# Cross-attention and expert layer on one core: overflow in groups of 64 slots, two tiles a step, second product on quarters of the array

## The chip, the cores and the metric

The kernel runs on one core of a Trainium2 chip. The metric is the device time of one execution in microseconds. Before the change the median of three runs is 230.85 us (230.7 to 230.89).

## The reference

The input x is 4 sequences of 256 tokens with 256 features, so N = 1024 tokens. It first gets an attention-like term of 256 columns added. Then comes the layer that this change is about, on z, the normalised x:

```
logits = z @ Wr.T + 0.5 * dom            # 64 experts
_, topk_idx = top_k(logits + router_bias, 4)
combine = softmax scores of the chosen four, scaled to sum 1
g, u = z @ Wg[e], z @ Wu[e]              # 256 -> 64, each expert e
out  = sum over e of (silu(g) * u * combine[:, e]) @ Wd[e]
for i in range(2): out += (silu(z @ Sg[i]) * (z @ Su[i])) @ Sd[i]   # shared, 256 -> 256 -> 256
```

Each token goes to four of the 64 experts, so there are 4096 pairs of token and expert, 64 an expert on average. Everything is float32.

## The kernel before

The attention term, the normalisations, the transposed z (`zT`), the logits and the choice of experts come first (up to about 50 us of the trace). In that time SP's queue brings in all expert weights. `codes`, `one_hot`, `list_tokens` and `tokens` then turn the choices into lists of tokens, one column of 128 slots for each tile. Each round of a list is one `one_hot` on VectorE (DVE), one `value` on ScalarE (ACT) and eight products on TensorE (PE, line 987).

A tile is 128 rows of z. There are two kinds:

- 32 *pair* tiles (NP). Slots 0 to 63 hold the first 64 tokens of expert 2q, slots 64 to 127 those of expert 2q + 1.
- *Overflow* tiles for what an expert has beyond 64 tokens, each 128 slots of one expert, whose number is known only at run time. They run in turns of four (U).

What a tile goes through, in the function `step` of each engine:

- POOL gathers its rows from `z_rows` in DRAM into `xg`, a ring of four (line 362 for pairs, 374 for overflow).
- PE transposes them in two pieces (line 1017). DVE copies them to `xgT` (line 810).
- PE multiplies by gate and up weights: line 1050 for a pair, in which each expert uses one half of the array's columns, line 1054 for overflow, on the whole array, with the expert's number in a register. Each float32 product is two instructions.
- ACT makes the silu (line 499). DVE multiplies by the up part (line 824, or 829 with the expert's parity, so that the right half of two stacked `wd` matrices is hit).
- PE transposes h (lines 1073, 1075), ACT copies it to `hT` (line 508), and PE makes the second product of 256 columns (line 1086).
- ACT copies y to `ysb`, a ring of four (line 518), and SP stores it to `y_slots` (lines 285, 291).

`over_tiles` writes the order out by hand: in one step the engines transpose tile s, do gate/up of tile s-1, turn h of tile s-2 and do the second product of tile s-3. The first 32 + 8 steps are written out, the others are a loop. Other work is put into certain steps: the second list of tokens for overflow (steps 1 to 12), `pick_choice` on DVE (line 773, two a step in steps 13 to 28).

When all y are stored, POOL gathers the 32 sets of result rows (`y_slots` to `z`, line 394, ring of eight), and DVE adds each with its weight (line 864). Beside this PE does the rest of the shared experts: `unit` (line 928) and `shared_out` (line 1122). Two of eight units are done before the tiles. SP stores the result in eight pieces.

## Time and profile before

| | |
|---|---|
| median of 3 runs | 230.85 us |
| span of the profiled execution, first to last instruction | 213.5 us |
| what lies around the span, against the median | 17.35 us |
| PE busy in the span | 173.6 us |
| POOL busy | 111.2 us |
| pair tiles, overflow tiles | 32, 28 |

The profiled execution is shown by its span alone; the runs are timed without it, and their median stands beside the span. Times in the trace count from the span's start. A row of a timeline is a start, a duration and a group of merged instructions; matmuls are pipelined and their ends modelled, so the distance between starts tells what the engine spends. "issue" is idle time that no recorded event explains. PEclk gives the granted clock of PE in tenths of full speed.

### The profile page before, as it was taken

To read this page: it belongs to the slowest core of one execution; us is meant where nothing else is said; L and a number is where in the kernel's file an instruction comes from. 1 tells how busy PE (TensorE), PEld (TensorE's weight loads), DVE (VectorE), ACT (ScalarE), POOL (GpSimd) and SP (SyncE) were. 2 spreads that over 40 slices of the span, in tenths; PEclk is the share of its full clock that TensorE was granted. 3 is DMA by queue.
4 is the path that set the end of the run, shared out by engine and by line. 5 is a ranking of instruction groups with operands and counts; after the bars stand their busy time and mean duration, and the time that the engine had idled before them with its cause. 6 is when DMAs were issued, how large, how long until landed. Compare 5 with 4: busy or idle time off the path is not lost.

```text
span 213.5 us, 4117 instructions
## 1 busy us (share of the span) xinstructions
PE 173.6 (81%) x963; PEld 124.0 (58%) x965; DVE 133.0 (62%) x528; ACT 88.4 (41%) x270; POOL 111.2 (52%) x121
## 2 busy tenths in 40 slices
PE   0990288999889999999999979999989979978300
PEld 0460178735536887777778968888844367436200
DVE  2999970467877655998997746666531440486450
ACT  2627496416224664555555636555551110210000
POOL 6595110010276535666665766666303777677740
PEclk9999999999655999999999999999999999999975
DMA  6899999997023432455544343443322333344431
GB/s 141 242 384 350 350 352 366 380 365 259 2 75 93 119 112 87 134 155 145 146 129 126 112 133 88 136 125 104 120 98 74 101 98 98 87 127 142 124 119 66
DMA packets 29825, 34.50 MB, mean 162 GB/s; under 512 B 4248, under 2 KB 27561, under 8 KB 29680
## 3 DMA queue, kind: packets, MB, share of 16 engines
q1 hardware_dynamic: 25392, 25.90, 36.8%
q0 software_dynamic: 4416, 8.41, 15.2%
q8 instruction: 7, 0.11, 0.3%
q14 instruction: 10, 0.08, 0.1%
HBM read 27.99 MB, written 9.96 MB: 178 GB/s over the span
## 4 chain that ended last, share of the span: by engine, by line
PE 66%; DVE 13%; ACT 6%; issue 4%; POOL 4%; DMA 3%; SPq 1%; POOLq 1%; DVEq 0%; ACTq 0%
PE pb L1086 13%; PE pb L928 13%; PE pb L1050 10%; PE pb L1017 7%; PE pb L1054 6%; PE pb L1073 4%; PE pb L1122 3%; POOL z L394 3%; PE pb L987 3%; DMA xs<-in_x 2%; PE pb L1075 2%; DVE sc L563 2%; DMA z<-y_slots,slot_i 1%; ACT z L428 1%; DVE sc L557 1%
## 5 line engine op out<-in xcount | busy, mean ns | idle before, releaser
L362 POOL DMA_INDIRECT xg<-z_rows,tok x32 | 32.9, 1029 | 29.3 <-issue 11.6
L394 POOL DMA_INDIRECT z<-y_slots,slot_i x32 | 32.5, 1016 | 21.4 <-DMA y_slots<-ysb 11.3
L1086 PE MATMUL pb<-wd_sb,hT 128*128 128x256 f32 (+1 forms) x120 | 37.5, 396 | 0.0
L374 POOL DMA_INDIRECT xg<-z_rows,tok_now x28 | 27.9, 997 | 14.3 <-issue 11.5
L928 PE MATMUL pb<-zT,shared_sb 128*128 128x512 f32 x64 | 32.3, 658 | 0.7 <-ACT ysb L518 0.7
L810 DVE COPY xgT<-pb 128x256 f32<-128x256 f32 x60 | 25.3, 422 | 11.4 <-PE pb L1017 10.4
L518 ACT ACTIVATE ysb<-pb 128x256 f32<-128x256 f32 x60 | 23.0, 383 | 12.1 <-PE pb L1086 11.1
L1017 PEld LDWEIGHTS pb<-ident,xg 128*128 128x128 f32 x120 | 22.6, 198 | 8.3 <-issue 5.1
L1017 PE MATMUL pb<-ident,xg 128*128 128x128 f32 x120 | 25.3, 294 | 1.9 <-issue 1.3
L499 ACT ACTIVATE sg<-pb 128x64 f32<-128x64 f32 x60 | 13.4, 223 | 29.8 <-PE pb L1050 18.9
L1050 PE MATMUL pb<-wgu_sb,xgT 128*64 128x128 f32 x256 | 22.4, 299 | 0.3 <-DVE xgT L810 0.3
L864 DVE SCALAR_TENSOR_TENSOR xs<-z,wgt,xs 128x256 f32<-128x256 f32 x32 | 15.4, 482 | 10.6 <-DMA z<-y_slots,slot_i 8.7
L928 PEld LDWEIGHTS pb<-zT,shared_sb 128*128 128x128 f32 x64 | 12.8, 206 | 15.5 <-issue 15.3
L1086 PEld LDWEIGHTS pb<-wd_sb,hT 128*128 128x128 f32 x120 | 19.9, 206 | 1.7 <-issue 0.6
L829 DVE SCALAR_TENSOR_TENSOR hh<-sg,parity,pb 128x64 f32<-128x64 f32 x56 | 13.2, 277 | 9.5 <-ACT sg L499 9.0
L469 ACT ACTIVATE qkT<-pb 128x512 f32<-128x512 f32 x8 | 4.8, 597 | 33.6 <-PE pb L928 33.6
L1122 PE MATMUL pb<-shared_sb,hsh 128*128 128x256 f32 x64 | 14.6, 384 | 4.3 <-DVE hsh L794 2.8
L1054 PE MATMUL pb<-wgu_sb,xgT 128*128 x112 | 17.7, 280 | 0.0
L824 DVE TENSOR_TENSOR hh<-sg,pb 64x64 f32<-64x64 f32 x64 | 13.9, 217 | 5.9 <-ACT sg L499 4.1
L508 ACT ACTIVATE hT<-pb 128x128 f32<-128x128 f32 x60 | 16.5, 276 | 2.4 <-PE pb L1075 1.0
L1050 PEld LDWEIGHTS pb<-wgu_sb,xgT 128*64 128x64 f32 x256 | 14.2, 144 | 4.9 <-DVE xgT L810 1.2
L1122 PEld LDWEIGHTS pb<-shared_sb,hsh 128*128 128x128 f32 x64 | 11.9, 190 | 7.8 <-DVE hsh L794 4.5
(165 smaller groups left out, 242.0 us busy)
## 6 DMA issues: line engine op xcount, KB each, us to landing
wgu_sb<-in_wgu SPq DMA_DIRECT2D x8, 1024.0 KB, 10.9
y_slots<-ysb SPq DMA_DIRECT2D x60, 128.0 KB
wd_sb<-in_wd SPq DMA_DIRECT2D x4, 1024.0 KB, 12.0
shared_sb<-in_shared SPq DMA_DIRECT2D x1, 1536.0 KB, 9.7
xs<-in_x SPq DMA_DIRECT2D x4, 256.0 KB, 4.4
z_rows<-z SPq DMA_DIRECT2D x4, 256.0 KB, 9.0
out<-xs SPq DMA_DIRECT2D x8, 128.0 KB, 1.8
xg<-z_rows,tok POOLq DMA_INDIRECT x32, 3.0
```

What stands on the lines that cost most here:

```text
L362: g.indirect_dma_start(xg[:, n, :], None, z_dram, bass.IndirectOffsetOnAxis(ap=tok[:, t:t + 1], axis=0), bounds_check=N - 1, oob_is_err=Fa ...
L374: g.indirect_dma_start(xg[:, n, :], None, z_dram, bass.IndirectOffsetOnAxis(ap=tok_now[:, n:n + 1], axis=0), bounds_check=N - 1, oob_is_er ...
L394: g.indirect_dma_start(z[:, j % NC, :].bitcast(I32), None, y_dram, bass.IndirectOffsetOnAxis(ap=slot_i[:, 0, j:j + 1].bitcast(U32), axis=0 ...
L508: a.activation(hT[:, n, :], pb[7][:, 0:P], ACT.Identity).then_inc(hT_sb, 1)
L518: a.activation(ysb[:, n, :], pb[4 + m % 2][:, 0:D], ACT.Identity).then_inc(y_sb, 1)
L810: v.tensor_copy(xgT[:, n, :, :], pb[n][:, 0:D].rearrange("p (c n) -> p c n", c=DC)).then_inc(xT_sb, 1)
L928: ins = t.matmul(pb[2 * (n % 2) + g][:, :], sgu_sb[:, i, g, h, hc * P:(hc + 1) * P], zT[:, h, blk * 512:(blk + 1) * 512], start=(h == 0), ...
L1017: ins = t.transpose(pb[n][:, h * P:(h + 1) * P], xg[:, m, h::DC], ident[:, :])
L1050: ins = t.matmul(pb[2 + n][h, 0:2 * F], xgT[:, n, c, h], wgu_sb[:, 2 * q + g, c, :], start=(c == 0), stop=(c == DC - 1))
L1054: ins = t.matmul(pb[2 + n][:, 0:2 * F], xgT[:, n, h, :], wgu_sb[:, bass.ds(gu_of[k], 1), h, :].rearrange("p o f -> p (o f)"), start=(h == ...
L1086: t.matmul(pb[4 + n][:, 0:D], hT[:, n, :], wd_sb[:, q, :] if pair else wd_sb[:, bass.ds(d_of[k], 1), :].rearrange("p o d -> p (o d)"), sta ...
L1122: ins = t.matmul(pb[4 + i % 4][:, 0:D], hsh[:, q, i * P:(i + 1) * P], sd_sb[:, q, :], start=(q == 0), stop=(q == NSH * DC - 1))
```

## The change

- Overflow is counted in groups of 64 slots. An overflow tile holds two groups, each of its own expert, so that it has the same form as a pair tile. `parity` and the dynamic weight addresses on PE are gone. Instead the weights of a group's expert are loaded again from DRAM into a place of `w_sb` whose own expert is done. SP does that: in each of the first 18 double steps it loads two experts, 0.197 MB each.
- Gate/up weights and the second weights lie together in one tensor `w_sb` of 384 numbers an expert and partition. `Wd` is stored with its left 128 columns in partitions 0 to 63 and its right 128 columns in 64 to 127.
- Tiles are done two at a time (a double step d, ND2 = 24 of them written out: 16 of pairs, 8 of overflow). Then a loop of turns of two tiles, at least one. In step d PE does gate/up of d, transposes of d+2, the second product of d-1 and the turn of h of d. The loop's turns have no such staging.
- h is written twice side by side, so that its transpose stands in both halves of the partitions. The second product is done in quarters: 64 rows by 64 columns of the array each, 128 moving columns, four for a tile.
- y of two tiles is stored by one DMA of 256 KB, from a ring of three.
- The list of overflow tokens is made for 32 tiles in place of 64. Shared experts, result gathers and the final additions stay as they are.

Of the loops' bodies only the added lines are shown; the removed ones stand in the kernel above.

```diff
-MAXOV = 64
+OT = 16
+MAXOV = 32
+NG = 2 * MAXOV
+ND2 = (NP + OT) // 2
...
-U = 4
-HEAD = 2
-XB = 4
-YB = 4
-GU_LAG, D_LAG = 1, 3
+XD = 3
+XB = 2 * XD
+YD = 3
+GROUP_W = DC * 2 * F + D // 2
+G0, G1 = 0, DC * 2 * F
...
-        wgu_sb = sb("wgu_sb", [P, E, DC, 2 * F])
-        wd_sb = sb("wd_sb", [P, E // 2, D])
+        w_sb = sb("w_sb", [P, E, GROUP_W])
+        wgu_v = w_sb[:, :, G0:G1].rearrange("p e (c n) -> p e c n", c=DC)
...
+        xgT = sb("xgT", [P, 2, 2, DC, P])
+        sg = sb("sg", [P, 2, 2, F])
+        hh = sb("hh", [P, 2, 2, 2, F])
+        hT = sb("hT", [P, 2, 2, P])
+        ysb = sb("ysb", [P, YD, 2, D])
+        tok_now = sb("tok_now", [P, 2], U32)
...
+                sp.dma_start(w_sb[:, 8 * n:8 * (n + 1), :], w[8 * n:8 * (n + 1), :, :].rearrange("e p n -> p e n")).then_inc(ld_w[n], 16)
...
+            def store(at, ring):
+                return sp.dma_start(y_dram[at, :].rearrange("(i p) d -> p i d", p=P), ysb[:, ring, :, :].bitcast(I32))
+            def experts_of(place):
+                _, vals = nc.values_load_multi_w_load_instructions(
+                    group_e[0:1, place], engines=[mybir.EngineType.SP], min_val=0, max_val=E - 1,
+                    skip_runtime_bounds_check_because="VectorE has bounded the expert of every group by E - 1")
+                return list(vals)
+            def reload(entry, expert):
+                return sp.dma_start(w_sb[:, entry, :], w[bass.ds(expert, 1), :, :].rearrange("o p n -> p (o n)"))
+            for d in range(ND2):
+                sp.wait_ge(y_sb, d + 1)
+                store(slice(2 * d * P, 2 * (d + 1) * P), d % YD).then_inc(y_out[d % YD], 16)
+                if d == 0:
+                    sp.wait_ge(at_ok, 2)
+                if d < OT + 2 and d % 2 == 0:
+                    pair = experts_of(slice(2 * d, 2 * d + 4))
+                if d < OT + 2:
+                    for h in range(2):
+                        reload(2 * d + h, pair[2 * (d % 2) + h]).then_inc(ld_over[d // 2], 16)
             n_turns = turn_count(sp)
             with sp.Fori(0, n_turns) as turn:
+                sp.wait_ge(y_sb, turn + (ND2 + 1))
+                store(bass.ds(turn * (2 * P) + 2 * ND2 * P, 2 * P), ND2 % YD).then_inc(y_out[ND2 % YD], 16)
+                later = experts_of(bass.ds(turn * 4 + (2 * OT + 4), 4))
+                for h in range(4):
+                    reload(2 * OT + h, later[h]).then_inc(ld_over[OT // 2], 16)
+            sp.wait_ge(mixed, K)
+            sp.wait_ge(ld_over[OT // 2], n_turns * 64 + 64)
...
-            g.memset(tri_less[:, :], float(P)).then_inc(const_ok, 1)
+            g.memset(tri_less[:, :], float(HB)).then_inc(const_ok, 1)
...
-            for t in range(NP):
+            for t in range(2 * ND2):
                 n = t % XB
                 if t >= XB:
-                    pool.wait_ge(xT_ps, t - XB + 1)
-                g.indirect_dma_start(xg[:, n, :], None, z_dram, bass.IndirectOffsetOnAxis(ap=tok[:, t:t + 1], axis=0),
+                    pool.wait_ge(xT_ps, t // 2 - XD + 1)
+                if t == NP:
+                    pool.wait_ge(tok_step, 5)
+                which = tok[:, t:t + 1] if t < NP else tok_over[:, t - NP:t - NP + 1]
...
+            pool.wait_ge(xT_ps, ND2 - XD + 1)
+            turn_no = ctx.enter_context(pool.register("turn_no"))
+            pool.reg_mov(turn_no, 1)
             n_turns = turn_count(pool)
+            with pool.Fori(0, n_turns) as _:
+                pool.wait_ge(tok_set, turn_no)
+                pool.reg_add(turn_no, turn_no, 1)
+                for i in range(2):
+                    n = 2 * (ND2 % XD) + i
+                    g.indirect_dma_start(xg[:, n, :], None, z_dram, bass.IndirectOffsetOnAxis(ap=tok_now[:, i:i + 1], axis=0),
+                                         bounds_check=N - 1, oob_is_err=False).then_inc(got[n], 16)
+            for n in range(YD):
+                more = n_turns * 16 if n == ND2 % YD else 0
+                pool.wait_ge(y_out[n], more + 16 * ((ND2 - 1 - n) // YD + 1))
+            last_row = n_turns * (2 * P) + (2 * ND2 * P - 1)
...
+            def gate(d, n):
+                act.wait_ge(gu_ps, d + 1)
+                a.activation(sg[:, n, :, :], pb[2 + n][:, 0:4 * F].rearrange("p (i f) -> p i f", i=2)[:, :, 0:F], ACT.Silu).then_inc(silu_ok, 1)
+            def evac_hT(d, n):
+                act.wait_ge(hT_ps, d + 1)
+                a.activation(hT[:, n, :, :], pb[2 + n][:, 256:512].rearrange("p (i n) -> p i n", i=2), ACT.Identity).then_inc(hT_sb, 1)
+            def evac_y(d, ring):
+                act.wait_ge(y_ps, d + 1)
+                for i in range(2):
+                    ins = a.activation(ysb[:, ring, i, :].rearrange("p (h c) -> p h c", h=2), banks[:, 4:6, i * P:(i + 1) * P], ACT.Identity)
+                ins.then_inc(y_sb, 1)
+            for d in range(ND2):
+                if d >= 2:
+                    act.wait_ge(h_ok, d - 1)
+                gate(d, d % 2)
+                if d >= 1:
+                    if d > YD:
+                        act.wait_ge(y_out[(d - 1) % YD], 16 * ((d - 1) // YD))
+                    evac_y(d - 1, (d - 1) % YD)
+                if d >= 2:
+                    act.wait_ge(y_ps, d - 1)
+                evac_hT(d, d % 2)
+                if d < NR:
+                    value(d, MAXOV, NR)
+            act.wait_ge(y_out[(ND2 - 1) % YD], 16 * ((ND2 - 1) // YD))
+            evac_y(ND2 - 1, (ND2 - 1) % YD)
+            n_turns = turn_count(act)
+            with act.Fori(0, n_turns) as turn:
+                d, n, ring = turn + ND2, ND2 % 2, ND2 % YD
+                act.wait_ge(h_ok, d)
+                gate(d, n)
+                act.wait_ge(y_ps, d)
+                evac_hT(d, n)
+                act.wait_ge(y_out[ring], turn * 16 + 16 * (ND2 // YD))
+                evac_y(d, ring)
...
-                v.tensor_scalar(need[:, 0, :], pb[5][0:E, 0:P], 1.0 / P, 0.5 - (0.5 + HB) / P, ALU.mult, ALU.add).then_inc(need_ok, 1)
+                v.tensor_scalar(need[:, 0, :], pb[5][0:E, 0:P], float(HB), -HB + 0.5 * HB - 0.5, ALU.max, ALU.add).then_inc(need_ok, 1)
                 dve.wait_ge(need_ok, 1)
-                v.tensor_scalar(need_bf[:, :], need[:, 0, :], ROUND, -ROUND, ALU.add, ALU.add).then_inc(need_ok, 1)
+                v.tensor_scalar(need[:, 1, :], need[:, 0, :], 1.0 / HB, ROUND, ALU.mult, ALU.add).then_inc(need_ok, 1)
+                dve.wait_ge(need_ok, 2)
+                v.tensor_scalar(need_bf[:, :], need[:, 1, :], -ROUND, None, ALU.add).then_inc(need_ok, 1)
...
+                v.tensor_scalar(turns_f[:, :], pb[5][0:1, 260:261], 0.25, 0.375 - OT / 2, ALU.mult, ALU.add).then_inc(turns_step, 1)
...
+            def group_experts():
                 dve.wait_ge(expert_ps, 1)
                 dve.wait_ge(at_ok, 1)
+                v.tensor_scalar(group_e[:, 0:NG], pb[7][0:1, 0:NG], float(E - 1), None, ALU.min).then_inc(at_ok, 1)
...
+            def evac_xT(d, n):
+                dve.wait_ge(xT_ps, d + 1)
+                v.tensor_copy(xgT[:, n, :, :, :].rearrange("p i c n -> p (i c n)"), pb[n][:, :]).then_inc(xT_sb, 1)
+            def hidden(d, n):
+                dve.wait_ge(silu_ok, d + 1)
+                up = pb[2 + n][:, 0:4 * F].rearrange("p (i f) -> p i f", i=2)[:, :, F:2 * F]
+                for k in range(2):
+                    ins = v.tensor_tensor(hh[:, n, :, k, :], sg[:, n, :, :], up, ALU.mult)
+                ins.then_inc(h_ok, 1)
+            evac_xT(0, 0)
+            evac_xT(1, 1)
+            for d in range(ND2):
+                if d >= 2:
+                    dve.wait_ge(hT_ps, d - 1)
+                hidden(d, d % 2)
+                if d + 2 < ND2:
+                    dve.wait_ge(gu_ps, d + 1)
+                    evac_xT(d + 2, d % 2)
+                if d == 0:
+                    group_experts()
+                if d < NR:
+                    one_hot(d, MAXOV, lanes, NR, NP)
+                if d == NR:
                     dve.wait_ge(lexp_ok, 1)
                     dve.wait_ge(z_out, 16 * B)
                     v.tensor_reduce(zden[:, 0, :], logit[:, :, :], AX.X, ALU.add).then_inc(w_step, 1)
                     tokens(tok_over[:, 0:MAXOV], pb[6][:, 192:192 + MAXOV], MAXOV, 2 * NR, 3)
                     dve.wait_ge(tok_step, 5)
+                    v.tensor_copy(tok_now[:, :], tok_over[:, OT:OT + 2]).then_inc(tok_set, 1)
+                if NR < d <= NR + NJ // 2:
+                    pick_choice(2 * (d - NR - 1))
+                    pick_choice(2 * (d - NR - 1) + 1)
+                if d == NR + NJ // 2 + 1:
                     weights_of_choices()
+            n_turns = turn_count(dve)
+            with dve.Fori(0, n_turns) as turn:
+                d, n = turn + ND2, ND2 % 2
+                dve.wait_ge(gu_ps, d)
+                evac_xT(d, n)
+                v.tensor_copy(tok_now[:, :], tok_over[:, bass.ds(turn * 2 + (OT + 2), 2)]).then_inc(tok_set, 1)
+                dve.wait_ge(hT_ps, d)
+                hidden(d, n)
...
+            def split_x(d, n, ring):
+                for i in range(2):
+                    for h in range(DC):
+                        ins = t.transpose(pb[n][:, (i * DC + h) * P:(i * DC + h + 1) * P], xg[:, 2 * ring + i, h::DC], ident[:, :])
+                ins.then_inc(xT_ps, 1)
+            def gate_up(d, n, entry):
+                for i in range(2):
+                    for c in range(DC):
+                        for h in range(2):
+                            own = slice(h * HB, (h + 1) * HB)
+                            ins = t.matmul(pb[2 + n][own, i * 2 * F:(i + 1) * 2 * F], xgT[:, n, i, c, own], wgu_v[:, entry + 2 * i + h, c, :],
+                                           start=(c == 0), stop=(c == DC - 1), skip_group_check=True)
+                ins.then_inc(gu_ps, 1)
+            def turn_h(d, n):
+                for i in range(2):
+                    ins = t.transpose(pb[2 + n][:, 256 + i * P:256 + (i + 1) * P], hh[:, n, i, :, :].rearrange("p k f -> p (k f)"), ident[:, :])
+                ins.then_inc(hT_ps, 1)
+            def down(d, n, entry):
+                for i in range(2):
+                    for h in range(2):
+                        own = slice(h * HB, (h + 1) * HB)
+                        for r in range(2):
+                            rows = slice(r * HB, (r + 1) * HB)
+                            ins = t.matmul(pb[4 + r][own, i * P:(i + 1) * P], hT[rows, n, i, own], w_sb[rows, entry + 2 * i + h, G1:],
+                                           start=True, stop=True, skip_group_check=True)
+                ins.then_inc(y_ps, 1)
+            def entry_of(d):
+                return 4 * d if d < NP // 2 else 4 * d - 2 * NP
+            def x_here(d):
+                for i in range(2):
+                    pe.wait_ge(got[2 * (d % XD) + i], 16 * (d // XD + 1))
             pe.wait_ge(unit_sb, 2)
+            x_here(0)
+            split_x(0, 0, 0)
+            x_here(1)
+            split_x(1, 1, 1)
+            pe.wait_ge(unit_sb, 2 * EARLY)
+            for d in range(ND2):
+                pe.wait_ge(xT_sb, d + 1)
+                if d >= 2:
+                    pe.wait_ge(hT_sb, d - 1)
+                if d < NP // 2:
+                    if d % 2 == 0:
+                        pe.wait_ge(ld_w[d // 2], 16)
+                else:
+                    pe.wait_ge(ld_over[d - NP // 2], 64)
+                gate_up(d, d % 2, entry_of(d))
+                if d + 2 < ND2:
+                    x_here(d + 2)
+                    split_x(d + 2, d % 2, (d + 2) % XD)
+                if d >= 1:
+                    pe.wait_ge(hT_sb, d)
+                    if d >= 2:
+                        pe.wait_ge(y_sb, d - 1)
+                    down(d - 1, (d - 1) % 2, entry_of(d - 1))
+                pe.wait_ge(h_ok, d + 1)
+                turn_h(d, d % 2)
+                if d == 0:
                     pe.wait_ge(cmp_ok, 2)
+                    pe.wait_ge(slot_ok, 1)
+                    t.matmul(pb[7][0:1, 0:NG], ones_bf[0:E, 0:1], cmp[:, :], start=True, stop=True,
                              skip_group_check=True).then_inc(expert_ps, 1)
+                if 1 <= d <= NR:
+                    list_tokens(d - 1, MAXOV, NR, 192)
+            pe.wait_ge(hT_sb, ND2)
+            pe.wait_ge(y_sb, ND2 - 1)
+            down(ND2 - 1, (ND2 - 1) % 2, entry_of(ND2 - 1))
+            n_turns = turn_count(pe)
+            with pe.Fori(0, n_turns) as turn:
+                d, n = turn + ND2, ND2 % 2
+                for i in range(2):
+                    pe.wait_ge(got[2 * (ND2 % XD) + i], turn * 16 + 16 * (ND2 // XD + 1))
+                pe.wait_ge(xT_sb, d)
+                split_x(d, n, ND2 % XD)
+                pe.wait_ge(ld_over[OT // 2], turn * 64 + 64)
+                pe.wait_ge(hT_sb, d)
+                pe.wait_ge(xT_sb, d + 1)
+                gate_up(d, n, 2 * OT)
+                pe.wait_ge(h_ok, d + 1)
+                turn_h(d, n)
+                pe.wait_ge(turns_step, 3)
+                pe.wait_ge(hT_sb, d + 1)
+                pe.wait_ge(y_sb, d)
+                down(d, n, 2 * OT)
+            end = n_turns + ND2
+            pe.wait_ge(xT_sb, end)
+            pe.wait_ge(hT_sb, end)
...
+                if blk == 0:
+                    pe.wait_ge(y_sb, end)
...
+        "w": np.concatenate([np.stack([L0_ffn_Wg.reshape(E, P, DC, F), L0_ffn_Wu.reshape(E, P, DC, F)], 3).reshape(E, P, -1),
+                             L0_ffn_Wd.reshape(E, F, 2, D // 2).transpose(0, 2, 1, 3).reshape(E, P, -1)], 2),
```

## Rows read from the trace of the kernel before

**Rows 1.** The page: busy time, clock by 40 slices, chain by engine.
```profile
PE 173.6 (81%) x963; PEld 124.0 (58%) x965; DVE 133.0 (62%) x528; ACT 88.4 (41%) x270; POOL 111.2 (52%) x121
...
PEclk9999999999655999999999999999999999999975
...
PE 66%; DVE 13%; ACT 6%; issue 4%; POOL 4%; DMA 3%; SPq 1%; POOLq 1%; DVEq 0%; ACTq 0%
```
**Rows 2.** Timeline of PE, 52 to 78 us: start, us, line, instructions merged into a row.
```profile
54.48 1.48 PE L987 MATMUL pb<-oh_val,sc 128*128 128x32 f16 x16 [0.62 <-DVE oh_tile L685]
...
62.70 1.12 PE L1050 MATMUL pb<-wgu_sb,xgT 128*64 128x128 f32 x8 [0.28 <-DVE xgT L810]
...
69.96 1.13 PE L987 MATMUL pb<-oh_val,sc 128*128 128x64 f16 x8
70.92 0.40 PE L1017 MATMUL pb<-ident,xg 128*128 128x128 f32 x2
71.25 0.66 PE L1050 MATMUL pb<-wgu_sb,xgT 128*64 128x128 f32 x8
71.83 0.33 PE L1073 MATMUL pb<-ident,hh 128*128 128x128 f32 x1
72.00 0.60 PE L1086 MATMUL pb<-wd_sb,hT 128*128 128x256 f32 x2
72.43 0.39 PE L1017 MATMUL pb<-ident,xg 128*128 128x128 f32 x2
```
**Rows 3.** Timeline of PE, 154 to 162 us.
```profile
154.24 0.27 PE L1075 MATMUL pb<-ident,hh 128*128 128x128 f32 x1
154.35 0.60 PE L1086 MATMUL pb<-wd_sb,hT 128*128 x2
154.78 0.39 PE L1017 MATMUL pb<-ident,xg 128*128 128x128 f32 x2
155.01 0.61 PE L1054 MATMUL pb<-wgu_sb,xgT 128*128 x4
155.46 0.27 PE L1075 MATMUL pb<-ident,hh 128*128 128x128 f32 x1
...
160.25 1.96 PE L928 MATMUL pb<-zT,shared_sb 128*128 128x512 f32 x4 [0.67 <-ACT ysb L518]
```
**Rows 4.** Timeline of POOL: the first gather of x and three gathers of results.
```profile
57.39 1.23 POOL L362 DMA_INDIRECT xg<-z_rows,tok  x1 [10.07 <-DVE tok L694]
...
162.98 1.00 POOL L394 DMA_INDIRECT z<-y_slots,slot_i  x1 [11.26 <-DMA y_slots<-ysb]
164.28 0.99 POOL L394 DMA_INDIRECT z<-y_slots,slot_i  x1 [0.30 <-issue]
...
204.66 0.99 POOL L394 DMA_INDIRECT z<-y_slots,slot_i  x1 [0.30 <-issue]
```
**Rows 5.** Groups by line, 80 to 116 us: busy us, mean ns of one, idle before.
```profile
L824 DVE TENSOR_TENSOR hh<-sg,pb 64x64 f32<-64x64 f32 x46 | 10.0, 217 | 2.7 <-ACT sg L499 1.5
L810 DVE COPY xgT<-pb 128x256 f32<-128x256 f32 x23 | 9.7, 423 | 2.3 <-PE pb L1017 1.7
...
L518 ACT ACTIVATE ysb<-pb 128x256 f32<-128x256 f32 x23 | 8.8, 383 | 3.6 <-PE pb L1086 3.6
...
L773 DVE SCALAR_TENSOR_TENSOR z<-slotmap,slot,logit 128x64 f32<-128x64 f32 x32 | 7.9, 282 | 0.5
...
L499 ACT ACTIVATE sg<-pb 128x64 f32<-128x64 f32 x24 | 5.4, 223 | 12.1 <-PE pb L1050 12.1
```
**Rows 6.** DMA queues, 92 to 112 us: packets, MB, share of 16 engines.
```profile
q0 software_dynamic: 649, 1.08, 25.2%
q1 hardware_dynamic: 1875, 1.71, 25.0%
```
**Rows 7.** DMA queue of SP, 14 to 50 us, the same columns.
```profile
q1 hardware_dynamic: 12871, 13.02, 109.0%
```
**Rows 8.** The chain in order of time: start, us, what.
```profile
125.46 1.32 issue
```

279 lines of the change are left out of this document (18 added, 261 removed).

## The prediction

> **What bounds the kernel now.** I began with the page. PE is busy 81% of the span and carries 66% of the chain that ended last; its clock digits are low only between about 59 and 75 us [rows 1]. The clock falls while PE waits around the listing of tokens, and comes back some microseconds after the expert tiles have begun.
>
> Then the timeline of PE. It shows three stretches after the routing. From 62.7 us on [rows 2] 32 pair tiles run, each two experts of 64 slots; then 28 overflow tiles of one expert each; from 160.25 us on [rows 3] the shared expert's products. In both tile stages PE has no real gap, so a tile costs what PE spends on it. One full-clock pair tile is the stretch from 70.92 to 72.43 us [rows 2]: starts 0.33, 0.58, 0.17 and 0.43 us apart, 1.51 us together. One overflow tile is 154.24 to 155.46 us [rows 3]: 0.11, 0.43, 0.23, 0.45, together 1.22 us. The second is easy to read: a float32 product is two instructions, 4 of 128 columns take 0.45 us and 2 of 256 take 0.43, so 128 columns are a slot of 0.107 us; a transpose is one slot. 11 slots are 1.18 us and 0.04 us is left over. The pair tile has 8 gate/up instructions of 128 columns on 64 columns of the array. One after the other they would take 0.86 us alone; they start within 0.58 us. So the two halves of the array work side by side: 4 slots, 0.43 us. The tile is again 11 slots, 1.18 us, and the other 0.33 us is the price of going from the whole array to halves and back.
>
> Behind PE, at nearly the same pace, stands POOL. Its gathers cannot follow each other faster than every 1.30 us (162.98 and 164.28) [rows 4]. And the end of the kernel hangs on POOL too: the 32 gathers of results begin at 162.98 us, once the last tile is stored, the last starts at 204.66 [rows 4], and the span ends 8.8 us after that. PE's own last stage runs beside them. So I take it that the end moves by what the first result gather moves.
>
> **The number of tiles.** Routing the reference's inputs gives 27 overflow tiles of 128 slots (before runs them in turns of 4, hence 28) and 35 groups of 64. After runs 16 overflow tiles, 32 groups, in the written-out part and one turn of two tiles for the other 3. That is 50 tiles for 60: 24 double steps and one turn.
>
> **One double step on PE.** Gate/up: 16 instructions in 8 side-by-side slots, 0.86 us. Four transposes of x: 0.43. Two of h: 0.21. The second product is 16 instructions of 128 columns on quarters of the array. Before shows no quarter. Serial they are 16 slots, 1.71 us; as halves 8 slots, 0.86; all four side by side 4 slots, 0.43. The half-array rows [rows 2] overlap fully and here the row halves write to different banks, so I take 0.43. The order halves, whole, quarters, whole has four changes, twice a pair tile's two: 0.66 us. Sum 2.59 us, against 3.02 for two pair tiles and 2.44 for two overflow tiles: per tile the overflow stage gains nothing; the gain is the 10 tiles and, in the pair stage, half of the second product.
>
> What may stand in the way of it in a step:
> - h. From the end of gate/up to the turn of h lie: 0.2 us until ACT starts, a silu of 128 elements (0.22 for 64, I take 0.28), two DVE products of 128 elements (0.22 each for 64, 0.54 together) and some 0.15 of handing over, 1.17 us. PE has 1.12 us of other work meanwhile (transposes, second product, changes). Some 0.1 us stays open: 2.70 us.
> - POOL: 2 gathers, 2.60 us, just under. The ring of three double tiles lets it run ahead.
> - DVE: copy of 512 columns 0.69 (0.42 for 256), products 0.54, two choices 0.72 [rows 5]: under 2.0 us. ACT: 0.28, two y copies of 0.38 and one of h, under 1.5 us [rows 5]. Both hidden by PE, with over half a microsecond of cover.
> - DMA. In the pair stage stores and gathers take 25.0% and 25.2% of the engines [rows 6], which is 1.52 us in the 3.02 us of two tiles. Added are, for the first 18 double steps, two expert blocks of 197 KB. The first loads bring 13.02 MB in 36 us, 362 GB/s [rows 7]; so 1.09 us. Together 2.61 us. That is a third resource at the same pace, and full. Reloads share SP's queue with the stores: a late store holds back ACT three steps on, then PE. The loads themselves are not wanted for 8 steps or more. I put the wait at 0 to 0.4 us a step and take nothing, as the double step is 0.1 longer than the demand.
> - SP: per step a store and two reloads instead of two stores, and it waits for each step's y first; nobody but its own queue stands behind that wait. Reading four expert numbers every other step is hidden.
>
> **The beginning.** Before starts gate/up at 62.70 us, after the first two gathers (57.39 us on). After transposes two double tiles first, so four gathers must have landed: the fourth starts about 4 us after the first and lands 3 us later, 65 us. With four transposes at half clock gate/up begins at about 66 us. The first two steps run wholly or mostly at half clock (gate/up 1.7 us, everything else doubled), as in before the rise came 5 to 6 us after 62.7. Adding them up I get the gate/up of the third double tile at about 75 us; before had then begun its seventh tile (about 75.2). So the start costs one double tile, near 3 us. Token listing: 4 rounds of 8 products, 0.96 us for 64 columns (69.96 to 70.92) and some 0.7 for 32 (54.48, 16 in 1.48) [rows 2]; three lie behind 75 us, 2.1 us.
>
> **The end.** 75.0 + 22 x 2.70 + 2.1 + 1.2 (the last second product, no longer covered) = 137.7 us. The turn isn't pipelined: each engine reads the count, which cost PE 1.32 us of issue at the old loop's start [rows 8], I take 1.0; transposes 0.43, copy 0.9, gate/up 0.96, silu 0.5, products 0.64, h 0.3, its copy 0.6, second product 0.53, y copies 0.96: 6.8 us. Then 3.2 us for a store twice as large (about 3.0 now) until the first result gather, at 147.7 us. Before: 162.98. Gain 15.3 us. The reference is the profile's span of 213.5 us; the median of the runs, 230.85 us, lies 17.35 us above it, which I leave as it is: 198.2 + 17.35 = 215.5 us. Ends for each unknown: per 0.1 us of step 2.2 us; second product between 0.43 and 0.86, up to +9.5 us (serial 1.71, +28); DMA wait up to 0.4 on 16 steps, +6.4; beginning +-2; turn 5 to 8 us.
>
> **Rivals.**
> 1. *The second product overlaps only in halves, or the weights of four quarters load in turn.* Step 3.13 us, so +9.5: 225 us. For: there are as many weight loads as products, and 4 of each would have to start within 0.107 us. Against: in the half-array stretch the loads start in pairs too. Chance 0.14.
> 2. *DMA is the bound while reloading.* Loads, stores and gathers together may move less than each alone: 3.05 us for 16 steps, 221 us. For: the demand of 2.61 us, and no stretch of before has all three at full share. Against: nothing needs these loads soon. Chance 0.15.
> 3. *Slower: the supply of PE instructions.* After has 38 weight loads and 38 products a double step, before 26 of each for two pair tiles in 3.02 us, that is 116 ns a couple; an overflow tile has 9 in 1.22 us. If 116 ns were the pace at which they can be supplied, a step would be 4.4 us and the kernel 37 us above my forecast, 253 us. It turns to a loss from a step of 3.4 us, 89 ns a couple. Against it: 8 couples start inside 0.58 us [rows 2], 73 ns each, and gaps stand only where the array mode changes. But those eight may have waited in a queue; no row shows 38 on end. Chance 0.08. A milder pace between 73 and 89 ns, say 3.08 us a step or 224 us, has 0.06. Serial quarters (step 3.98, 244 us) would end on the slow side too, chance 0.03.
> The Trainium skill bears on this place (TensorE: Matmul & The Clock Gate, Back-to-back issue gap): a lasting stream of loads and products of 128 columns is given as about 81 ns each. By that, an estimate from that page, 38 would be 3.08 us and the time some 224 us, the milder pace above; the half-array row beats it for eight, and no row tests it for longer.
> 4. *Better than forecast.* Some changes of mode hide, or the start loses nothing: POOL's 2.60 us then holds: 211 us. Chance 0.1.
>
> **Chances.** The forecast, a step of 2.6 to 2.85 us, 212 to 219 us: 0.44. All but rival 3 at its full price and serial quarters are faster than before. The range 210 to 227 takes in the forecast, rivals 1 and 2, the milder pace and most of 4; outside are rival 3, serial quarters and a rest of mishaps. A measurement can tell about 0.2%, 0.5 us, from no change; faster by more 0.87, within it 0.02, slower 0.11.
>
> **What would show it.** Second product: 16 instructions starting within 0.43 to 0.5 us (0.9 means rival 1). Double steps 2.7 us apart at full clock between 80 and 135 us; evenly longer with gaps before gate/up too is rival 3, longer only up to the 18th step with ACT or POOL waiting on DMA is rival 2. POOL's gathers close to 1.3 us apart all through. First result gather near 148 us and the same 50 us from there to the end. I am wrong if the tail grows, if the turn drops PE's clock for the shared expert's products, or if the first steps at half clock last longer than to 75 us.

## The result, and the profile after

| occasion | before | after | ratio, 95% interval |
|---|---|---|---|
| first comparison | 230.77 us (4 runs) | 220.32 us (219.29 to 221.47, 4 runs) | 0.9552, 0.95 to 0.9605 |
| fourth | 227.53 us | 217.78 us | 0.9541, 0.9456 to 0.9627 |
| sixth | 228.08 us | 218.36 us | 0.9619, 0.9559 to 0.9679 |

The kernel is 10.45 us faster where 15.35 was forecast. Sign and range (210 to 227 us) held, though 220.32 lies above the 212 to 219 of the forecast itself; the way to it did not hold. The span of the profiled execution of after is 218.0 us where the forecast's sum gave 198.2. What lies around the span is 2.0 us where the sum carried 17.35. So two errors, 19.8 us one way and 15.3 us the other, stood against each other, and that the time still lies in the range is luck.

The page of after, first its busy times, then the clock in 40 slices, then the chain by engine (answers to [rows 1]):

```profile
PE 153.2 (70%) x1245; PEld 104.9 (48%) x1246; DVE 105.0 (48%) x388; ACT 68.1 (31%) x190; POOL 101.6 (47%) x111
...
PEclk9999999999958889999999999999859999999755
...
PE 48%; DVE 13%; issue 10%; another core or an unknown queue 9%; ACT 8%; POOL 5%; DMA 5%; POOLq 1%; DVEq 0%; ACTq 0%
```

PE is down from 81% to 70% of a longer span: a kernel that PE bounded is now idle for a fifth of the stage of the double steps (PE busy 35.04 us of 45 between 80 and 125 us). The clock isn't the reason; the granted clock is 1.00 from 81 to 152 us. Where PE is not waiting, its parts are what the forecast said. The timeline of PE near the end of the stage (start, us, line; answers to [rows 2, 3]), and then the turn:

```profile
144.63 1.10 PE L1005 MATMUL pb<-w_sb,xgT 128*64 128x128 f32 x16
145.66 0.75 PE L996 MATMUL pb<-ident,xg 128*128 128x128 f32 x4
146.34 0.67 PE L1022 MATMUL pb<-w_sb,hT 64*64 64x128 f32 x16
146.93 0.44 PE L1012 MATMUL pb<-ident,hh 128*128 128x128 f32 x2
147.30 1.09 PE L1005 MATMUL pb<-w_sb,xgT 128*64 128x128 f32 x16
...
152.88 0.67 PE L1022 MATMUL pb<-w_sb,hT 64*64 64x128 f32 x16 [0.53 <-ACT hT L493]
154.54 0.74 PE L996 MATMUL pb<-ident,xg 128*128 128x128 f32 x4 [0.99 <-issue]
156.06 1.77 PE L1005 MATMUL pb<-w_sb,xgT 128*64 128x128 f32 x16 [0.78 <-DVE xgT L800]
158.79 0.69 PE L1012 MATMUL pb<-ident,hh 128*128 128x128 f32 x2 [0.96 <-DVE hh L807]
160.06 1.13 PE L1022 MATMUL pb<-w_sb,hT 64*64 64x128 f32 x16 [0.58 <-issue]
```

Gate/up 1.03 us, transposes 0.68, the second product on quarters 0.59 for 16 instructions, the turn of h 0.37: 2.67 us. But this step is an exception, and it stands behind the last gather of rows, which starts at 143.22 us. A dozen steps before it, all engines of one step in order of time:

```profile
100.74 1.00 POOL L362 DMA_INDIRECT xg<-z_rows,tok  x1 [1.34 <-PE pb L996]
...
101.29 1.09 PE L1005 MATMUL pb<-w_sb,xgT 128*64 128x128 f32 x16
...
102.04 1.00 POOL L362 DMA_INDIRECT xg<-z_rows,tok  x1 [0.30 <-issue]
...
102.32 0.75 PE L996 MATMUL pb<-ident,xg 128*128 128x128 f32 x4
...
103.00 0.67 PE L1022 MATMUL pb<-w_sb,hT 64*64 64x128 f32 x16
103.67 0.28 ACT L488 ACTIVATE sg<-pb 128x128 f32<-128x128 f32 x1 [1.83 <-PE pb L1005]
...
104.05 0.49 DVE L807 TENSOR_TENSOR hh<-sg,pb 128x128 f32<-128x128 f32 x2 [2.18 <-ACT sg L488]
104.41 1.00 POOL L362 DMA_INDIRECT xg<-z_rows,tok  x1 [1.37 <-PE pb L996]
...
104.59 0.44 PE L1012 MATMUL pb<-ident,hh 128*128 128x128 f32 x2 [0.93 <-DVE hh L807]
104.96 0.77 PE L1005 MATMUL pb<-w_sb,xgT 128*64 128x128 f32 x10
```

The step takes 3.67 us (101.29 to 104.96). PE leaves gate/up at about 102.4, yet ACT's silu starts at 103.67 and is said to have waited for exactly that. The recorded semaphore events show why: the increment at the end of gate/up lands at 103.59 us, those of the transposes and of the second product at 103.65 and 103.81. All come out together, 1.2 us late for the first. I call this a **late signal**: a group of matmuls whose increment is recorded over 0.1 us after its last matmul has ended. The counts below match increments with matmuls and can be off by some four, since records are missing. In this profile 45 of 66 are late between 80 and 140 us. In the profile of before that the forecast rests on it is 0 of 225 from 66 to 155 us. No increment of ACT or DVE is late in any profile in that stretch. In after itself the late signals end with the gathers of rows: from 145.7 to 165.9 us, between the last of these gathers and the first result gathers, none of 16 is late.

The end of the kernel, POOL's timeline (answers to [rows 4]), and the DMA queues from 92 to 112 us (answers to [rows 6]):

```profile
165.16 1.00 POOL L389 DMA_INDIRECT z<-y_slots,slot_i  x1 [20.94 <-DMA y_slots<-ysb]
...
190.04 1.19 POOL L389 DMA_INDIRECT z<-y_slots,slot_i  x1 [4.32 <-DVE xs L852]
...
210.02 1.00 POOL L389 DMA_INDIRECT z<-y_slots,slot_i  x1 [0.30 <-issue]
```

```profile
q1 hardware_dynamic: 3266, 3.82, 57.7%
q0 software_dynamic: 524, 0.95, 22.8%
```

The first result gather comes at 165.16 us, forecast 147.7. From there to the end it is 52.8 us, forecast 50.5; a stall of 4.3 us stands in it, in which POOL waits for DVE, DVE for ACT and ACT for the shared expert's products. PE and ACT of after there, then the same of before:

```profile
181.09 7.03 PE L916 MATMUL pb<-zT,shared_sb 128*128 128x512 f32 x16
188.06 1.08 ACT L464 ACTIVATE qkT<-pb 128x512 f32<-128x512 f32 x2 [14.75 <-remote]
```

```profile
179.21 10.46 PE L928 MATMUL pb<-zT,shared_sb 128*128 128x512 f32 x24
182.84 0.60 ACT L469 ACTIVATE qkT<-pb 128x512 f32<-128x512 f32 x1 [11.42 <-PE pb L928]
```

The first eight of these products end 3.6 us after their start in both. In before ACT follows at once (182.84 us). In after they end at 184.69, but their increment is recorded at 188.04: a late signal again, by 3.3 us.

### The profile page after: what moved, and what is told of

It reads as the page before. It is cut to its first block, busy times and chain, and to the rows that moved or that the text cites. A ratio compares the mean times of both kernels' runs of the same rounds, so it can differ in the third digit from the quotient of the medians.

```text
span 218.0 us, 3782 instructions
## 1 busy us (share of the span) xinstructions
PE 153.2 (70%) x1245; PEld 104.9 (48%) x1246; DVE 105.0 (48%) x388; ACT 68.1 (31%) x190; POOL 101.6 (47%) x111
## 3 DMA queue, kind: packets, MB, share of 16 engines
q0 software_dynamic: 3936, 8.40, 15.3%
## 4 chain that ended last, share of the span: by engine, by line
PE 48%; DVE 13%; issue 10%; another core or an unknown queue 9%; ACT 8%; POOL 5%; DMA 5%; POOLq 1%; DVEq 0%; ACTq 0%
PE pb L1005 20%; PE pb L916 9%; PE pb L1012 5%; POOL z L389 4%; DVE hh L807 3%; PE pb L996 3%; PE pb L1022 3%; ACT sg L488 2%; DVE xs L852 2%; DMA proj_sb<-in_proj 2%; PE pb L881 2%; PE pb L887 2%; PE pb L975 2%; DVE sc L565 2%
## 5 line engine op out<-in xcount | busy, mean ns | idle before, releaser
L807 DVE TENSOR_TENSOR hh<-sg,pb 128x128 f32<-128x128 f32 x50 | 12.2, 284 | 49.9 <-ACT sg L488 49.8
L1005 PE MATMUL pb<-w_sb,xgT 128*64 128x128 f32 x400 | 30.0, 295 | 0.8 <-DVE xgT L800 0.8
L1005 PEld LDWEIGHTS pb<-w_sb,xgT 128*64 128x64 f32 x400 | 23.4, 146 | 4.7 <-issue 3.2
L1012 PE MATMUL pb<-ident,hh 128*128 128x128 f32 x50 | 11.2, 306 | 18.9 <-DVE hh L807 14.2
L362 POOL DMA_INDIRECT xg<-z_rows,tok_over x16 | 15.9, 997 | 13.2 <-PE pb L996 10.8
L488 ACT ACTIVATE sg<-pb 128x128 f32<-128x128 f32 x25 | 6.9, 278 | 45.4 <-PE pb L1005 42.5
L852 DVE SCALAR_TENSOR_TENSOR xs<-z,wgt,xs 128x256 f32<-128x256 f32 x32 | 15.5, 483 | 11.3 <-DMA z<-y_slots,slot_i 9.8
L800 DVE COPY xgT<-pb 128x512 f32<-128x512 f32 x25 | 17.1, 685 | 7.6 <-PE pb L996 5.8
L996 PEld LDWEIGHTS pb<-ident,xg 128*128 128x128 f32 x100 | 14.6, 210 | 11.9 <-issue 11.7
L1099 PE MATMUL pb<-shared_sb,hsh 128*128 128x256 f32 x64 | 15.7, 403 | 6.1 <-DVE hsh L791 3.6
L1022 PE MATMUL pb<-w_sb,hT 64*64 64x128 f32 x400 | 17.3, 289 | 1.8 <-ACT hT L493 1.2
L1022 PEld LDWEIGHTS pb<-w_sb,hT 64*64 64x64 f32 x400 | 11.1, 137 | 5.5 <-issue 1.6
```

The lines of the kernel that those rows point to most:

```text
L362: g.indirect_dma_start(xg[:, n, :], None, z_dram, bass.IndirectOffsetOnAxis(ap=which, axis=0), bounds_check=N - 1, oob_is_err=False).then_ ...
L800: v.tensor_copy(xgT[:, n, :, :, :].rearrange("p i c n -> p (i c n)"), pb[n][:, :]).then_inc(xT_sb, 1)
L807: ins = v.tensor_tensor(hh[:, n, :, k, :], sg[:, n, :, :], up, ALU.mult)
L852: v.scalar_tensor_tensor(xs[:, i, :], z[:, j % NC, :], wgt[:, j:j + 1], xs[:, i, :], ALU.mult, ALU.add).then_inc(mixed, 1)
L996: ins = t.transpose(pb[n][:, (i * DC + h) * P:(i * DC + h + 1) * P], xg[:, 2 * ring + i, h::DC], ident[:, :])
L1005: ins = t.matmul(pb[2 + n][own, i * 2 * F:(i + 1) * 2 * F], xgT[:, n, i, c, own], wgu_v[:, entry + 2 * i + h, c, :], start=(c == 0), stop= ...
```

## The experiments

The runs fell on six occasions, and kernel before took 230.8, 231.1, 214.8, 227.5, 214.4 and 228.1 us (medians) on them; 214.8 and 227.5 are one and the same chip at two times. So every run below is read beside before on its own occasion.

### Before once more (e1)

No edit.

> The kernel before once more, to see how its profiled span and its own time go together: the first profile had a span of 213.5 us beside timed runs of 230.8, while the changed kernel's profiled execution had 218.0 us and 220.03. If the first profile was an unusually short execution, this one's span is near 228 us and the extra time lies in the tile loop (POOL or PE waits); if a profile always lacks it, the span is again 213 to 214 us.

Measured: 231.73 us, ratio 0.9992 (0.995 to 1.0033). Its profiled execution took 233.78 us with a span of 232.0. PE's timeline, in which the tiles of 1.51 us of [rows 2] are broken by waits, and the first result gather:

```profile
94.68 0.66 PE L1050 MATMUL pb<-wgu_sb,xgT 128*64 128x128 f32 x8
96.30 0.33 PE L1073 MATMUL pb<-ident,hh 128*128 128x128 f32 x1 [0.96 <-DVE hh L824]
96.46 0.60 PE L1086 MATMUL pb<-wd_sb,hT 128*128 128x256 f32 x2
96.90 0.39 PE L1017 MATMUL pb<-ident,xg 128*128 128x128 f32 x2
```

```profile
178.66 1.00 POOL L394 DMA_INDIRECT z<-y_slots,slot_i  x1 [13.82 <-DMA y_slots<-ysb]
```

56 of 147 signals are late here from 66 to 155 us. The result gathers begin 15.7 us later than in [rows 4]. From there to the end it takes 53.4 us, with the same stall as in after (a gather 4.91 us behind the one ahead of it, after a signal of the shared products that is 2.9 us late). So the profile that the forecast rests on is of an execution without late signals. The runs beside it took as long as the runs here, which have them. What lies around a span is 1.8 us (233.78 against 232.0), and I put the other 15.5 us of the 17.35 down to late signals; no trace of the runs beside the first profile was kept.

### Reloads out, gathers out (e2, e3)

e2 leaves out all 40 reloads of weights, so the overflow tiles compute with the weights that lie there.

```diff
-                if d < OT + 2:
-                    for h in range(2):
-                        reload(2 * d + h, pair[2 * (d % 2) + h]).then_inc(ld_over[d // 2], 16)
```

> The changed kernel without the 40 reloads of expert weights and without the waits on them (the overflow tiles use whatever weights lie in their places). Theory DMA (a full set of DMA engines slows the step from 2.7 to 3.65 us): steps fall to 2.7 to 2.9 us and the time to 204 to 207 us. Theory POOL (the step is locked to the two gathers of POOL, which end about 0.6 us before ACT goes on): steps stay at 3.6 us, time 218 to 220 us.

e3 leaves out the gathers after those of the first three double tiles, so later tiles compute on old rows.

```diff
-            for t in range(2 * ND2):
+            for t in range(XB):
```

> The changed kernel with the gathers of x done only for the first three double tiles; all later ones take the rows that lie in the ring (so most tiles compute on the wrong rows). Theory POOL: with no gathers running the step is 2.6 to 2.7 us, as the last three double steps of the changed kernel, time near 203 us. Theory DMA: the reloads and stores stay, so a step stays above 3.2 us; theory of array modes (PE's completions come late after its short bursts on halves and quarters): 3.6 us.

Measured on the same occasion: e2 220.8 us, so the DMA rival is out for these occasions, as the load of the engines fell from 81% to 43% (92 to 112 us) and the time did not. e3 196.28 us, ratio 0.8497 (0.8438 to 0.8556), below the 203 us expected and far from what the theories of DMA and of array modes asked for (steps above 3.2 us). Between 80 and 140 us no signal is late in e3, of 82, and 41 of 68 are in e2. The timeline of e3, PE and ACT:

```profile
100.35 1.09 PE L1001 MATMUL pb<-w_sb,xgT 128*64 128x128 f32 x16
...
101.55 0.28 ACT L484 ACTIVATE sg<-pb 128x128 f32<-128x128 f32 x1 [0.44 <-PE pb L1001]
...
102.65 0.44 PE L1008 MATMUL pb<-ident,hh 128*128 128x128 f32 x2
...
103.02 0.31 PEld L1001 LDWEIGHTS pb<-w_sb,xgT 128*64 128x64 f32 x6 [0.17 <-DVE xgT L796]
```

Silu starts 1.20 us after gate/up does (2.38 in after), PE never waits for h, and the step is 2.67 us. On this occasion late signals need the gathers. A ring of six double tiles for the rows (e4), which would have let POOL run further ahead, does not fit into SBUF, so there is no time for it.

### One more stage (e5, e10)

The turn of h goes one step later, the second product two steps behind gate/up. Nothing is left out.

```diff
                 gate_up(d, d % 2, entry_of(d))
+                if d >= 1:
+                    pe.wait_ge(h_ok, d)
+                    turn_h(d - 1, (d - 1) % 2)
                 if d + 2 < ND2:
...
-                    down(d - 1, (d - 1) % 2, entry_of(d - 1))
-                pe.wait_ge(h_ok, d + 1)
-                turn_h(d, d % 2)
+                    down(d - 2, d % 2, entry_of(d - 2))
```

> Kernel after with one more stage in its pipeline: turning h goes one step later and the second product two steps behind gate/up (PE's order in a step: gate/up(d), turn h(d-1), split x(d+2), second product(d-2)). Nothing is left out. Theory (completion signals of the PE that come about 1.2 us late beside a gather sit in the chain gate/up, silu, hidden, turn h, which PE waits for within the same step): with a step between them the late signal costs nothing, a double step falls from 3.65 us towards 2.7 to 2.9 us and the kernel to 205 to 209 us. Rival (the pace of a step is set by the gathers themselves, two at about 1.3 us each behind the signal of split x, so 3.65 us is POOL's loop): steps stay at 3.5 to 3.7 us and the time within 1 us of 220.

> The kernel with one more stage again, beside kernel after on the same chip. Theory (the extra stage hides a signal that is 1.2 us late): where before takes about 231 us, steps of 2.7 to 3.0 us and 204 to 210 us against 220 of after; where before takes about 215 us, 1 to 4 us less than after, because the 0.1 to 0.3 us that PE waits for h within a step go too. Rival (steps set by POOL's loop of signal and two gathers): within 1 us of after on either.

e5: 199.65 us beside a before of 214.82, ratio 0.9223 (0.9164 to 0.9282); no late signal in it, nor in any profile of that occasion. So the run can't tell the theories apart, and its time stands below my 205 to 209. e10, with late signals: 216.52 us, ratio 0.9505 (0.9441 to 0.9568), and after itself (e9) 217.78 beside it. My theory said 204 to 210, the rival "within 1 us of after"; the difference is 1.3 us and within the scatter of either. The theory that one more stage hides the late signals has fallen. PE's timeline of e10 shows that the wait only moved, to the copy of hT ahead of gate/up and to that of y:

```profile
101.72 0.67 PE L1027 MATMUL pb<-w_sb,hT 64*64 64x128 f32 x16 [1.86 <-ACT ysb L499]
102.39 1.09 PE L1010 MATMUL pb<-w_sb,xgT 128*64 128x128 f32 x16
...
106.08 1.09 PE L1010 MATMUL pb<-w_sb,xgT 128*64 128x128 f32 x16 [1.15 <-ACT hT L493]
```

What stays the same is how many gathers are issued. The view by windows, 80 to 125 us (length; busy time of PE, PEld, DVE, ACT, POOL with the number of instructions, for POOL the gathers; clock; DMA share; GB/s). Before, the profile that the forecast rests on:

```profile
80.00:125.00 45.00, 45.00 (x373) 36.32 (x373) 37.05 (x178) 25.90 (x91) 29.14 (x30) 1.00 0.45 129
```

Before (e1), after, e2 and e10, all beside late signals:

```profile
80.00:125.00 45.00, 41.39 (x344) 32.24 (x341) 32.74 (x165) 21.20 (x80) 25.52 (x26) 1.00 0.40 117
```

```profile
80.00:125.00 45.00, 35.04 (x484) 26.48 (x484) 19.14 (x82) 15.66 (x50) 25.02 (x26) 1.00 0.76 225
```

```profile
80.00:125.00 45.00, 37.14 (x500) 28.13 (x494) 19.85 (x85) 17.12 (x55) 25.30 (x25) 0.95 0.39 114
```

```profile
80.00:125.00 45.00, 34.72 (x511) 27.63 (x510) 21.02 (x89) 16.23 (x54) 24.99 (x26) 0.99 0.76 226
```

And e5, without late signals:

```profile
80.00:125.00 45.00, 40.85 (x609) 32.07 (x601) 25.87 (x112) 21.13 (x64) 32.41 (x34) 1.00 0.92 285
```

25 or 26 gathers in 45 us, 1.73 to 1.80 us each, in four different kernels, whether PE's work for a gather is 1.51 us (before), 1.33 (after) or 1.23 (e10). e9 has 26 too. The step shown above suggests how this comes about: POOL is a full ring ahead, so its next pair of gathers waits for the signal of the last transposes; that signal is held until 1.61 us after the start of the second gather (102.04 to 103.65); POOL starts 0.76 us later (104.41). 1.30 + 1.61 + 0.76 = 3.67 us, the step. By this reading the gathers hold back the signal that releases the next gathers, and PE's work fits inside the loop in either order tried. That the loop is closed in this way is read from the trace; no run opened it.

### A stage more and a bank of its own for the turned h (e11)

Again nothing is left out. On top of e5 the turned h goes to PSUM bank 7, and gate/up no longer waits for its copy.

```diff
-                    ins = t.transpose(pb[2 + n][:, 256 + i * P:256 + (i + 1) * P], ...
+                    ins = t.transpose(pb[7][:, i * P:(i + 1) * P], ...
```

> The kernel with one more stage, and h turned into PSUM bank 7, which has no other use by then, instead of the half of the gate/up bank; so gate/up(d) no longer waits for the copy of hT(d-2), and PE's order is gate/up(d), split x(d+2), turn h(d-1), second product(d-2). Nothing is left out. With the extra stage alone and late signals the steps stayed at 3.5 us, because PE waited 0.9 to 1.15 us before gate/up for the copy of hT, whose signal (of turn h) was late. Theory (every signal of PE is about 1.2 us late beside a gather, and a step is as long as the tightest loop through one): each loop now has 1.8 us or more between PE's end and its own next need, so beside late signals the steps are 2.5 to 2.9 us and the kernel takes 198 to 206 us where before takes 227 to 231; where before takes 215, 195 to 200 us. Rival (POOL's loop, signal of split x then two gathers, sets 3.5 us): still 214 to 218 us where before takes 227 to 231.

198.77 us beside a before of 214.36, ratio 0.9264 (0.9205 to 0.9322); one of its six runs took 420.49 us, which nothing here explains. No late signals on this occasion, so its purpose was missed. What it does show is the next bound without them; PE's timeline, then two rows of POOL's:

```profile
93.54 1.09 PE L1010 MATMUL pb<-w_sb,xgT 128*64 128x128 f32 x16
95.13 0.72 PE L1001 MATMUL pb<-ident,xg 128*128 128x128 f32 x4 [0.49 <-DMA xg<-z_rows,tok]
95.68 0.38 PE L1017 MATMUL pb<-ident,hh 128*128 128x128 f32 x2
95.99 0.67 PE L1027 MATMUL pb<-w_sb,hT 64*64 64x128 f32 x16
96.59 1.09 PE L1010 MATMUL pb<-w_sb,xgT 128*64 128x128 f32 x16
```

```profile
92.67 1.00 POOL L362 DMA_INDIRECT xg<-z_rows,tok  x1 [0.30 <-issue]
93.97 1.00 POOL L362 DMA_INDIRECT xg<-z_rows,tok  x1 [0.30 <-issue]
```

Steps are 2.52 us, now and then 3 and more where PE waits for gathered rows. From 80 to 103 us POOL issues its gathers 1.30 us apart without waiting for anybody, so two of them take 2.60 us and PE, at 2.52, catches up with them: that is the pace named in rival 4 of the forecast. The DMA engines are 94% busy between 80 and 125 us, so the DMA rival stands close behind; no run takes the two apart.

### What of a gather does it (e6, e12, e7)

e6 and e12 are one kernel: later gathers find every index but 0 out of bounds, so POOL works and hardly a row moves. e7 takes the gathers away and brings the same bytes by plain transfers on ACT's queue, not the chosen rows.

```diff
-                                     bounds_check=N - 1, oob_is_err=False)
+                                     bounds_check=N - 1 if t < XB else 0, oob_is_err=False)
```

```diff
                 gate(d, d % 2)
+                if d + XD < ND2:
+                    act.wait_ge(xT_ps, d + 1)
+                    for i in range(2):
+                        t = (2 * (d + XD) + i) % NT
+                        a.dma_start(xg[:, 2 * (d % XD) + i, :], z_dram[t * P:(t + 1) * P, :]).then_inc(row[...], 16)
```

> Kernel after, but from the seventh gather on every row index above 0 is out of bounds, so that POOL does all its work for a gather while next to no rows move (x is stale, results differ). If it is POOL's work at a gather (its descriptors) that holds PE's signals back: steps stay near 3.6 us, time 216 to 221 us. If it is the rows in flight: steps 2.67 us and 196 to 199 us, as without gathers.

> The kernel with empty gathers again, since at its first run no chip signal was late in any kernel. Where before takes 227 to 231 us: if POOL's work at a gather (its descriptors) holds the signals back, steps stay at 3.3 to 3.6 us and the time at 214 to 220 us; if the rows in flight do, steps 2.7 us and 196 to 199 us. Where before takes 215 us it is 197 us as at its first run and tells nothing.

> Kernel after, with the same bytes brought in by plain transfers of 128 rows in order, issued on ACT's queue, in place of the gathers from the seventh on (rows are not the chosen ones, results differ; the turn's gathers are left out). If the signals are late because of data landing in SBUF or the load on the DMA engines: steps stay at 3.3 to 3.7 us, time 214 to 221 us. If they are late because of what POOL does for a gather: steps 2.7 to 2.9 us (ACT has two more issues a step), time 197 to 203 us.

197.22 us, 197.24 us and 212.57 us (ratio 0.9893, 0.9839 to 0.9947), all on occasions on which the profiles show no late signals. So they don't answer the question, and it stays open whether POOL's work or the rows in flight hold the signals. e7 missed both expectations by something else: its transfers are asked for only behind silu and take 3.4 us to land, and PE waits for rows in most steps:

```profile
99.81 1.09 PE L1007 MATMUL pb<-w_sb,xgT 128*64 128x128 f32 x16
102.40 0.72 PE L998 MATMUL pb<-ident,xg 128*128 128x128 f32 x4 [1.50 <-DMA xg<-z_rows]
```

### Before without gathers (e8)

The gathers after the first four left out.

> Kernel before, gathers left out after the first four (x is stale, results differ). If late signals beside gathers also are what separates the execution profiled first (span 213.5 us) from the usual ones (some 229 to 232 us): no late signal, steps of 1.51 us throughout, time 212 to 216 us, so the change is worth 16 to 19 us where there are no gathers and 10.5 us beside them. If the difference has another cause: 222 us or more.

211.08 us, ratio 0.9832 (0.9789 to 0.9876) to a before of 214.82 on that occasion. That is a little below the 212 to 216 expected, and before itself took 214.82 on this occasion with its gathers, so the run doesn't test what separates the slower occasions from this one. Beside e6 (197.22, same occasion) it puts the change at 13.9 us where gathers don't matter.

### After twice more (e9, e13)

> Kernel after once more, unchanged. On the chip of the last four kernels, kernel before took 214.82 us (231 us in every run before that) and no completion signal of the PE in any of their profiles was late. Theory (late signals are a matter of the chip that a run falls on, and only there do gathers bring them): where before takes about 231 us, after takes 219 to 222 us with steps of 3.65 us; where before takes about 215 us, after has no late signal, steps of 2.7 us and 198 to 202 us. Rival (only the clock or the reloads set the 3.65 us): after takes about 220 us, or 3 to 6 per cent less than before, on either kind of chip.

> Kernel after, unchanged, in the hope of an occasion on which no signal is late: so far it has only been timed beside late signals (220.3 and 217.8 us, steps of 3.65 us), and the forecast's sum was made on a profile of before that has none. Theory: where before takes about 215 us, after has no late signal, steps of 2.7 us and takes 199 to 202 us, as the sum has it (a span of 198.2 us and 1.9 us around it): 13 to 15 us less than before. Where before takes 227 to 231 us: 217 to 221 us again. Rival (the 3.65 us steps have another cause in kernel after): 212 us or more even where before takes 215.

217.78 and 218.36 us, late signals both times (48 of 97 and 44 of 96 from 66 to 155 us), steps of 3.6 us; the first is 1.2 us under the 219 to 222 expected. After was never run on an occasion without late signals, so the part of both expectations that would have told the theory from its rival was not reached. That it takes some 200 us there, as the sum has it, is what e3, e5 and e6 (196.28, 199.65 and 197.22 us) suggest; it isn't shown.

## Why the prediction was right or wrong

**The size of the gain, wrong by 5 us.** By the sum 15.3, measured 10.45, 9.75 and 9.7.

**"the median of the runs, 230.85 us, lies 17.35 us above it, which I leave as it is": this is the step that failed.** A span and its own time differ by 1.7 to 2.1 us in every run here. A gap of 17.35 said that the profile and the runs were not of the same kind, and the rows of PE (no gap in 60 tiles) were not those of a kernel that takes 230.85 us. The constant hid some 15.5 us that no row of that profile shows, and I let them stand for after too. After pays about as much: its first result gather comes 17.5 us later than the sum had it, that of before (e1) 15.7 us later than in the profile the sum was made on. That is why a sum made as a difference still came within 5 us. Profile against profile (233.78 and 220.03 us) the gain is 13.75 us, but e1's profiled execution lies 2 us over its own median, so how the 5 us that are missing from the gain divide up stays open.

**Where the 19.8 us of span went.** The third double tile's gate/up was forecast at 75.0 us and came at 74.57. From there the written-out part was to end at 137.7; it ended at about 153.5, 15.8 us later. The 2.70 us of a step is the term of the sum that was too small: of the 21 step distances 14 lie between 3.4 and 3.9 us. The turn took 7.7 us (152.88 + 0.6 to 161.2) for 6.8, with the clock at 0.74 of full in 152 to 161 us: gate/up 1.77 us where it takes 1.10 at full clock. The stretch to the first result gather took 4.0 for 3.2. The tail took 2.4 more, the stall of POOL.

**h, "some 0.1 us stays open".** The wait for h is 0.9 us in a step. The chain itself was sized well: in e3 silu starts 1.20 us after the start of gate/up, 0.1 us after its last product has ended, and PE finds h ready. What I had no term for is the signal from PE to ACT.

**Second product, "so I take 0.43".** Right. The 16 instructions take 0.60 us with a change of array mode; they start in fours, the fours 0.11 to 0.14 us apart, all within 0.40 us (after, 103.00 to 103.39 us). Rival 1 (0.9 us) is out, and so are serial quarters. Page "TensorEngine Tiling (Array Packing)" of the Trainium skill, Key Properties, says that different tiles can load weights and multiply in parallel and that changing the mode drains the array; the trace agrees on both: the four parts of the step exceed their slots by 0.17, 0.25, 0.16 and 0.16 us, 0.74 together where I put 0.66, and e5, which has its two whole-array parts next to each other and so one change fewer, has steps of 2.47 us where PE doesn't wait.

**Rival 3, the supply of PE instructions.** Out. 38 couples take 2.67 us, 70 ns each, changes of mode included, and the 16 on quarters 38 ns each. The Trainium skill (TensorE: Matmul & The Clock Gate, Back-to-back issue gap) gives about 81 ns for 128 columns in a lasting stream, by which the step would be 3.08 us, an estimate from that page; by these rows the figure doesn't bind couples that lie on halves and quarters of the array.

**Rival 2, DMA.** Out beside late signals (e2: 220.8 us without reloads). Without them it is close, 92 and 94% busy in e5 and e11, but there POOL's gathers are at their own pace of 1.30 us, which alone can make PE wait for rows.

**"POOL: 2 gathers, 2.60 us, just under."** Right as a rate (1.30 us a gather in e11), wrong as an independence. I took POOL's loop as free of PE's since it runs ahead. It does run ahead, and by the reading above that is why it waits on PE's newest signal, which comes 1.61 us after the start of its own last gather.

**The tail, "the same 50 us".** 52.8 us. The shared expert's products did start on a slower clock (0.50 granted until 163.1 us), and their first stretch took 1.0 us longer (161.12 to 174.08 us, in before 160.25 to 172.20). But the stall of POOL comes from a signal 3.3 us late, and before has it too beside late signals (e1: 53.4 us), so it is no cost of the change. Of my signs of being wrong, the tail that grows and the dropped clock came true; how much of the missing gain the clock holds stays open.

## What to carry to other kernels

Compare a profile's span with its own time before building on it: a gap of 17 us where 2 are usual says that the rows shown are not those of the runs. Where several engines hang on one engine's signals beside gathers, count gathers and not only work: here each cost 1.73 to 1.80 us in four kernels, and another order of the same work in e10 gained nothing that can be told from the scatter. The kernel with the added stage is 7.8% faster than before where signals are on time (e5) and 5.0% where they are late (e10). What the stage itself adds where signals are on time is not known, since after was never run there. And look behind the bound that falls: in e11 it was POOL's 1.30 us a gather.

## What was not expected of the hardware

PE's semaphore increments can come out together, 1.2 us late and more, in after mostly 1.5 to 1.8 us after the start of the last gather, while those of ACT and DVE are on time. With gathers left out it was 0 of 82 (e3) where 41 of 68 were late with them (e2), on one occasion; in e3 late signals come back beside the result gathers, three of nine. On other occasions no kernel shows it, on the same chip too, and before then takes 214 to 215 us, not 227 to 231. The Trainium skill (TensorE: Matmul & The Clock Gate, The cost: per-tile semaphore tail) tells of increments that wait on each other at some 26 ns each; nothing near 1.2 us, so that isn't it. What sets the occasion, and whether POOL's work or the rows in flight do it, is open.
